# Re-planning the last blocks of an LSTM + state-space kernel, with a polynomial logarithm and one scan per piece

## The reference

```python
def layer0(x, h0, Wx, Wh, b):            # LSTM over 512 steps, hidden 512
    xW = x @ Wx + b
    for t in range(512):
        i, f, o, g = split(xW[:, t] + h @ Wh)        # sigmoid, sigmoid, sigmoid, tanh
        c = f * c + i * g
        h = o * tanh(c)
def layer1(x, conv_w, conv_b, Wp, bp, Ws, bs, A_log, dt_log, Wo, bo):   # conv_w = cond, 8 taps
    conv = conv_b + sum(x_pad[:, k:k + L] * conv_w[k] for k in range(8))
    proj = conv @ Wp + bp
    B, C = softplus(proj[..., :64]), tanh(proj[..., 64:])
    u = x @ Ws + bs
    decay = 1 - softplus(dt_log) * softplus(A_log)
    state[t] = decay * state[t-1] + softplus(dt_log) * B[t] * u[t]
    return (C * state) @ Wo + bo
x = x + layer0(x, cond, ...)
out = x + layer1(x, cond[:, None], ...)
```

## Time and profile before

| | |
|---|---|
| median of 3 runs | 1922.39 us (1920.68 to 1922.65) |
| profiled execution | 1919.75 us |
| its span, first to last instruction | 1917.8 us |
| granted TensorE clock, mean | 0.995 |
| busy: PE, PE weight load, DVE, ACT, POOL | 94%, 74%, 72%, 53%, 18% |

### The profile page before, as it was taken

One profiled execution on the slowest core, in us unless ns is written; L12 is line 12 of the kernel. 1 busy time (PEld: TensorE's weight loads), 2 busy tenths in 40 slices (PEclk: granted clock), 3 DMA queues, 4 the chain that ended last, 5 costly groups with the idle time before them and its releaser, 6 DMA issues.

```text
span 1917.8 us, 123272 instructions
## 1 busy us (share of the span) xinstructions
PE 1810.3 (94%) x52690; PEld 1419.5 (74%) x52690; DVE 1388.6 (72%) x6911; ACT 1015.9 (53%) x4057; POOL 337.5 (18%) x1544
## 2 busy tenths in 40 slices
PE   5888999999999999999999999999999999999976
PEld 3666777777777777777777777777777777777865
DVE  8677667777677776777777677777777777867675
ACT  5555455555555555555555545555555555545442
POOL 1111111111111111111111111111111111111110
PEclk9999999999999999999999999999999999999998
DMA  6111111111111211111111111111111121211100
GB/s 236 53 42 38 48 54 37 51 55 44 53 51 39 63 43 54 44 50 55 48 57 40 54 54 42 59 45 51 53 53 45 46 56 40 74 38 50 46 15 24
DMA packets 112668, 100.81 MB, mean 53 GB/s; under 512 B 20353, under 2 KB 86453, under 8 KB 111094
## 3 DMA queue, kind: packets, MB, share of 16 engines
q1 hardware_dynamic: 111704, 90.79, 15.6%
q10 hardware_dynamic: 416, 2.13, 0.3%
HBM read 50.90 MB, written 41.94 MB: 48 GB/s over the span
## 4 chain that ended last, share of the span: by engine, by line
PE 78%; DVE 10%; ACT 5%; issue 3%; POOL 2%; DMA 1%; SPq 0%; ACTq 0%; POOLq 0%; DVEq 0%
PE recA L540 28%; PE recB L534 24%; PE pw L501 12%; PE pbc L585 10%; DVE tr L900 4%; ACT act L783 3%; POOL h L468 2%; DVE hz L931 2%; DVE pre L906 2%; DVE prod L914 1%; ACT tc L793 1%; PE pw L485 1%; PE po L605 1%; PE pu L558 1%; DMA wpk<-in_L_cond_Wh_dram 1%
## 5 line engine op out<-in xcount | busy, mean ns | idle before, releaser
L783 ACT ACTIVATE act<-pre 128x64 f32<-128x64 f32 x1024 | 262.7, 257 | 854.3 <-DVE pre L909 838.1
L540 PE MATMUL recA<-whi,hz 128*16 128x256 f16 x8176 | 516.0, 275 | 75.6 <-DVE hz L931 62.3
L534 PE MATMUL recB<-whi,hz 128*32 128x128 f16 x16352 | 577.6, 219 | 0.4 <-issue 0.4
L534 PE MATMUL recB<-wlo,hz 128*32 128x128 f16 x16352 | 577.6, 219 | 0.1
L540 PE MATMUL recA<-wlo,hz 128*16 128x256 f16 x8176 | 512.6, 273 | 0.0
L534 PEld LDWEIGHTS recB<-whi,hz 128*32 128x32 f16 x16352 | 438.0, 97 | 10.2 <-issue 0.6
L534 PEld LDWEIGHTS recB<-wlo,hz 128*32 128x32 f16 x16352 | 437.9, 97 | 2.6 <-issue 0.2
L540 PEld LDWEIGHTS recA<-whi,hz 128*16 128x16 f16 x8176 | 199.9, 88 | 303.5 <-DVE hz L931 281.6
L900 DVE STREAM_TRANSPOSE tr<-recA 128x256 f32<-128x256 f32 x512 | 230.0, 449 | 203.5 <-PE recA L540 201.6
L585 PE MATMUL pbc<-yt,wpk 128*128 128x256 f32 (+5 forms) x1120 | 329.6, 400 | 0.0
L468 POOL TENSOR_TENSOR h<-osc,tc 128x16 f32<-128x16 f32 x1024 | 226.3, 221 | 465.4 <-ACT tc L793 465.4
(11 more groups left out here) (157 smaller groups left out, 1989.8 us busy)
## 6 DMA issues: line engine op xcount, KB each, us to landing
xw_rows<-xs SPq DMA_DIRECT2D x128, 256.0 KB, 2.5
seed<-xw_rows SPq DMA_DIRECT2D x1008, 32.0 KB, 2.0
xn<-in_x_dram SPq DMA_DIRECT2D x32, 256.0 KB
out_dram<-ot SPq DMA_DIRECT2D x32, 256.0 KB, 3.0
seed<-in_L_cond_Wh_dram ACTq DMA_DIRECT2D x2, 1024.0 KB, 6.6
wpk<-in_L_cond_Wh_dram SPq DMA_DIRECT2D x2, 1024.0 KB, 12.2
wlo<-in_L_cond_Wx_dram SPq DMA_DIRECT2D x2, 1024.0 KB, 13.7
xs<-in_L_cond_Wx_dram SPq DMA_DIRECT2D x1, 1024.0 KB, 10.0
```

Source lines behind the costliest of these rows:

```text
L534: ins = pe.matmul(rec[1][32 * j:32 * j + 32, 0:128], h[:, k, 2 * NB * (1 - c):2 * NB * (1 - c) + 32], w[:, k, 4 * (2 + c) + j, :], start=F ...
L540: ins = pe.matmul(rec[0][32 * j:32 * j + 2 * NB, 0:256].rearrange("p (c f) -> p c f", c=2), h[:, k, 2 * NB:4 * NB], w[:, k, :, :].rearrang ...
L783: act_eng.activation(act[q][:, 0:G, :].rearrange("p g n -> p (g n)"), pre[q][:, :, :, :].rearrange("p g c b -> p (g c b)"), ACT.Tanh, scal ...
```

## The change

1. **Planning.** Blocks 12 and 13, block 14 and piece 15 get plans of their own (`NEAR_END`: conv parts, first `y_u` step, first step of the ScalarE ops, `room`). `MANY` is gone: VectorE ops go by booked costs everywhere, with a table of costs for 128-column pieces.
2. **Conv in halves.** Blocks 13 and 14 convolve 16 steps (128 columns) at a time: 64 jobs in place of 32, the first half starting before the block's y is complete. Other jobs per piece stay 32.
3. **y of the last step alone.** `output` runs for steps 508 to 510 at step 510 and for 511 alone (32 columns), and the last conv is split in three: what needs y to 507 (32 jobs), to 510 (16 jobs, issued at step 511), and step 511 (4 jobs of 8 columns). `y_u` of a piece is issued behind conv in `beside`; for the last piece it comes after the 4 jobs, and `abs`, `sig` go ahead of `u` on ScalarE.
4. **Polynomial logarithm.** log(1+e^-|z|) = -log(1-s) is a polynomial of degree 10 in s: `den`, `rcp`, `w`, `w2` go, terms rise from seven to nine.
5. **One scan for all batches.** `drive` writes `acc` batch-major (a transposed view), `carry` adds decay times the state before to the first step of each batch, and `dec` holds 0 there, so that one scan runs through several batches: 128 columns each, so two scans for a block and one for a 16-step piece in place of eight. `ys` reads the state through a transposed view.
6. The outputs of blocks 0 to 11 come out at other steps, since `ys` does; the first half of block 15 is put out at 509, T and T+1 (residual, the two matmuls), the second half after it.

```diff
-        DVE_COST = {"den": 0.33, "rcp": 0.46, "w": 0.34, "w2": 0.34, "top": 0.34, "term": 0.44, "sum": 0.44,
-                    "drive": 0.44, "scan": 0.2, "ys": 0.35}
+        DVE_COST = {"top": 0.34, "term": 0.44, "sum": 0.44,
+                    "drive": 0.44, "carry": 0.1, "scan": 0.4, "ys": 0.35}
+        DVE_COST_HALF = {"top": 0.25, "term": 0.32, "sum": 0.32, "drive": 0.38, "carry": 0.2, "scan": 0.46, "ys": 0.3}
...
         def conv_order(i):
             n, a, e, cols = span(i)
+            taps = [(c, k) for k in range(TAPS) for c in range(KC)]
+            if i < LAST - 1:
+                return [(c, k, a, e) for c, k in taps]
             if i < NP - 1:
-                return [(c, k, a, e) for k in range(TAPS) for c in range(KC)]
-            reach = [min(e, e - HS + TAPS - 1 - k) for k in range(TAPS)]
-            return ([(c, k, a, reach[k]) for k in range(TAPS) for c in range(KC)] +
-                    [(c, k, reach[k], e) for k in range(TAPS) for c in range(KC) if reach[k] < e])
...
+                return [(c, k, lo, lo + TT) for lo in range(a, e, TT) for c, k in taps]
+            order, done = [], [a] * TAPS
+            for last in (e - HS, e - 1, e):
+                reach = [min(e, last + TAPS - 1 - k) for k in range(TAPS)]
+                order += [(c, k, done[k], reach[k]) for c, k in taps if done[k] < reach[k]]
+                done = reach
+            return order
...
+        NEAR_END = {LAST - 2: ([(0, 8, 3, 1), (8, 32, 11, 2)], 11, 23, 0.65),
+                    LAST - 1: ([(0, 64, -5, 3)], 10, 17, 0.65),
+                    LAST: ([(0, 32, -12, 3), (32, 64, 0, 3)], 4, 11, 0.9),
+                    LAST + 1: ([(0, 32, 0, 7)], 2, 5, 0.8)}
...
+            if i == NP - 1:
...
+                conv_when[i] = [(0, late[0], T - HS, (late[0] + HS - 1) // HS), (late[0], final[0], T - 1, jobs),
+                                (final[0], jobs, T, jobs)]
+                u_when[i] = [T] * KC
+                post_at[i] = [T + 1] * len(post_order(i))
...
-                    pe_load[first + (j - lo) // rate] += 0.46
+                    pe_load[first + (j - lo) // rate] += 0.46 if span(i)[3] == COLS and i < LAST - 1 else 0.23
...
                 if name == "drive":
                     dve.wait_ge(s_sp, i + 3)
                     dve.wait_ge(s_usb, i + 1)
-                    dve.scalar_tensor_tensor(sp[:, 0:cols], sp[:, 0:cols], dtv[:, 0:1], us[:, 0:cols],
-                                             ALU.mult, ALU.mult).then_inc(s_drive, 1)
+
+                    dve.scalar_tensor_tensor(by_batch(acc[:, 0:cols]), by_step(sp[:, 0:cols]), dtv[:, 0:1],
+                                             by_step(us[:, 0:cols]), ALU.mult, ALU.mult).then_inc(s_drive, 1)
+                elif name == "carry":
+
+                    if i:
+                        dve.wait_ge(s_drive, 2 * i)
+                        dve.wait_ge(s_scan, i)
+                        ahead = pieces[i - 1][2] - pieces[i - 1][1]
+                        first = acc[:, 0:cols:e - a]
+                        dve.scalar_tensor_tensor(first, st[:, (i - 1) % 2, ahead - 1:NB * ahead:ahead], decay[:, 0:1], first,
+                                                 ALU.mult, ALU.add).then_inc(s_drive, 1)
                 elif name == "scan":
...
+                    some = slice(128 * z, 128 * z + 128)
+                    ins = dve.tensor_tensor_scan(st[:, i % 2, some], dec[0 if e - a == TB else 1][:, :], acc[:, some], 0.0,
                                                  ALU.mult, ALU.add)
```

More of the change, by code:

```diff
@@ L190, in span, with y_steps, y_done @@
             return n, a, e, NB * (e - a)
+        def y_steps(t):
+            if t == T - 2:
+                return list(range(T - HS, T - 1))
+            if t == T - 1:
+                return [t]
+            return list(range(t - HS + 1, t + 1)) if (t + 1) % HS == 0 else []
+        def y_done(t):
+            return t // HS + 1 if t < T - 1 else T // HS + 1
         def conv_order(i):
             n, a, e, cols = span(i)
+            taps = [(c, k) for k in range(TAPS) for c in range(KC)]
+            if i < LAST - 1:
+                return [(c, k, a, e) for c, k in taps]
             if i < NP - 1:
[L197 to L205 removed]
+                return [(c, k, lo, lo + TT) for lo in range(a, e, TT) for c, k in taps]
[5 more added lines that the diff above has]
+            return order
         def soft_order(key):
[L208 removed]
+            return ["abs", "sig", "pos"], ["top"] + ["term"] * SERIES + ["sum"]
         def post_order(i):
             on_act, on_dve = soft_order(i + 2)
[L212 removed]
+            on_act = ["u"] + on_act + ["c"] if i < NP - 1 else ["abs", "sig", "u", "pos", "c"]
+            return on_act + on_dve + ["drive", "carry"] + ["scan"] * (span(i)[3] // 128) + ["ys"]
         par_order = sum(soft_order(0), []) + ["dtv"] + sum(soft_order(1), []) + ["dtv", "decay"]
@@ new lines, in lstm_ssm_kernel @@
+            base = TB * n + e
+            if i == NP - 1:
+                late = [j for j in range(jobs) if y_done(TB * n + min(e, conv_order(i)[j][3] + conv_order(i)[j][1] - TAPS + 1) - 1)
+                        > (T - HS) // HS]
+                final = [j for j in late if conv_order(i)[j][3] + conv_order(i)[j][1] - TAPS + 1 == e]
+                conv_when[i] = [(0, late[0], T - HS, (late[0] + HS - 1) // HS), (late[0], final[0], T - 1, jobs),
+                                (final[0], jobs, T, jobs)]
+                u_when[i] = [T] * KC
+                post_at[i] = [T + 1] * len(post_order(i))
+                slot = T + 2
+                continue
@@ new lines, in lstm_ssm_kernel @@
+            if i in NEAR_END:
+                conv_plan, u_first, slot, room = NEAR_END[i]
+                conv_when[i] = [(lo, hi, base + first, rate) for lo, hi, first, rate in conv_plan]
+                u_when[i] = [base + u_first + k for k in range(KC)]
+                slot += base
+            else:
+                conv_when[i] = [(0, 13, base + 3, 1), (13, 21, base + 16, 2), (21, jobs, base + 20, 1)]
+                u_when[i] = [base + 27 + k for k in range(KC)]
+                slot, room = base + 31, 0.65
@@ new lines, in lstm_ssm_kernel @@
+            act_at = ACT_AT if e - a == TB else {"u": 0, "abs": 0, "sig": 0, "pos": 1, "c": 1}
+            post_at[i] = [slot + act_at[name] for name in post_order(i)[:len(act_at)]]
+            slot += max(act_at.values())
+            for name in post_order(i)[len(act_at):]:
+                cost = (DVE_COST if e - a == TB else DVE_COST_HALF)[name]
+                while dve_load[slot] + cost > room:
+                    slot += 1
+                dve_load[slot] += cost
+                post_at[i].append(slot)
@@ L265, in lstm_ssm_kernel @@
+            slot += 3 if i not in NEAR_END else 0
+            for z in range(2):
+                if TT * z < e and a < TT * z + TT and (a <= TT * z):
+                    slot = min(slot + 3, T - 1)
                     while evacuates(slot):
                         slot += 1
[L267 to L287, removed]
+                    out_when[n, z] = (slot - 2, slot - 1, slot) if e - a == TB else (slot - 2, T, T + 1)
@@ L611, in beside @@
                 for i in range(NP):
+                    for lo, hi, first, rate in conv_when[i]:
+                        for j in due(t, first, rate, hi - lo):
+                            conv(i, lo + j)
                     for k in range(KC):
@@ L1058, in _ @@
             dve.memset(ys[N:N + 1, :, :], 1.0).then_inc(s_ones, 1)
-            dve.memset(dec[:, :], 1.0).then_inc(s_dec, 1)
+            for z in range(2):
+                dve.memset(dec[z][:, :], 1.0).then_inc(s_dec, 1)
+            dve.wait_ge(s_dec, 2)
+            for z in range(2):
+                dve.memset(dec[z][:, 0:128:TB >> z], 0.0).then_inc(s_dec, 1)
             for q in range(2):
```

107 lines of the change are left out of this document (35 added, 72 removed).

## The result

The changed kernel takes 1926.10 us (median of 22 runs, 1923.18 to 1928.76), the kernel before in the same sessions 1921.93 (22 runs, 1919.99 to 1927.47). The ratio is 1.0022, 95% interval [1.0016, 1.0027]: slower by 4.2 us, where I had forecast 1.3 us less, and above the high end of my range, 1925.0.

A forecast was written before the change was run, and what follows sets the result against it. A loop through VectorE, ScalarE and GpSimd sets the floor, TensorE the fuller steps; 10.5 + 1.5 - 10.8 - 2.5 = -1.3 us on the median 1922.39 gives 1921.1, range 1910.5 to 1925.

The forecast's parts named there:

- The threshold: Each step: side work is free down to a floor of 3.56 us, until TensorE's jobs overfill it; 0.03 us room.
- the lists: Jobs of each step worked out from the code, priced by trace durations to tell which steps exceed the floor.
- the middle costs nothing: Rival: fuller steps before the end cost no time, so its gain of 13.3 stays; 1910.6 us, chance 0.14.
- half of it: Rival: the additional job costs, but steps with output matmuls stay at the floor; 1915.8 us, chance 0.12.
- my likeliest case: Whole kernel: no change by the bound of 0.2%, 1921.1 us, own range 1918 to 1924, chance 0.67.
- The middle: Even groups 6 to 26: outputs moved earlier pack TensorE's steps fuller, 0.96 us per group, 11 groups: +10.5 us.
- Steps 416 to 479: Steps with half conv jobs or two conv jobs come to 5.5 us over the floor, in place of 4.0: +1.5.
- The end: Steps 480 to 510: gains of 2.6, 7.2 and 1.0 us in three stretches, together -10.8.
- the half clock stretch: Steps 493 to 507: TensorE's stretch at half its clock goes, since no step keeps it idle as long.
- The tail: From step 511's conv on: gains of 0.6 before `abs`, 1.24 in the series, 0.7 after `drive`; -2.5 us, give or take 1.
- My 0.115 a record: Last conv in the tail: price of each TensorE record in us, putting the end of 56 records at 1903.6.
- The transposed view: `drive`'s strided write on VectorE: bounds 0 and 1 ns a column; 0 taken, 0.5 us kept for the range.

The follow-up runs named there:

- the first kernel: The changed kernel with `y_u` issued ahead of the conv jobs again, except for the last piece; 1922.61 us, ratio 0.9999 to the kernel before.
- the third: The changed kernel with `y_u` ahead of conv and the outputs of blocks 0 to 10 at the steps of the kernel before; 1913.70 us, ratio 0.9949.
- fifth: The third with the last conv in two parts in place of three; 1911.11 us, ratio 0.9943 to the kernel before.
- the ninth: The fifth with 64 waits more on VectorE at its start; 1912.62 us, ratio 0.9941 to the kernel before.

## Why the prediction was wrong

**The threshold was right.** A step costs nothing until TensorE's jobs fill it, and the earlier trace rows showed 0.03 us of room. Five projections gave 3.67 (forecast 3.68), two conv jobs, or a conv and an output job, with three 3.63 to 3.65 (forecast 3.64), in the very steps that the lists named. Moving `ys`, and with it the outputs, cost 11.3 in the kernel with the polynomial alone and 9.9 in the first, against my 10.5. In the changed kernel it is 10.7: its 13.0 less the 2.3 of `y_u` below. The rivals "the middle costs nothing" and "half of it" are refuted by the same rows.

**The step that failed is the costing of one edit in the third part of the change, "`y_u` of a piece is issued behind conv".** It has no term in my sum. My lists counted each job of a step at its own duration, `y_u` at 0.37 wherever it stands, so that an exchange of two neighbours in one queue cost nothing. It costs 0.2 in every step where `y_u` and a later wide job are at the threshold: one of `y_u`'s four steps in each of the 11 blocks (219: 3.77, with `y_u` ahead 3.57), 428 to 430 and others. In steps 64 to 415 that is 11 x 0.21 = 2.3. The table's 13.0 - 9.9 = 3.1 has 0.8 more, since the first kernel's profile has a floor 0.007 higher, and the steps that TensorE fills are as long in both. In 416 to 479 it is 1.1 (428 to 430 and 458 to 460), in 480 to 492 0.6: 4.0 in all, of the 7.6 by which the two spans differ from the forecast. By the medians the first experiment gives back 3.5 of the missing 5.5, and without this one reordering the change measures 1922.6, inside the range of my likeliest case (1918 to 1924).

**The middle, +15.0 for 10.5.** 13.0 of it is in the table, 2.3 of that `y_u`'s; 2.0 is pauses, 0.5 of them VectorE's at 128n + 63 and 1.3 in steps 186 and 187, where the chain of the changed kernel shows issue, a wait for nothing that the profile shows, within recB:

```profile
721.41 0.33 PE recB L549 x21
721.74 0.55 issue
722.29 0.68 PE recB L549 x35
```

The first kernel loses 0.8 in the same two steps, the third and fifth 0.2 in 187, the others nothing; what such a stop is stays open.

**Steps 416 to 479, +3.1 for 1.5.** 1.1 of the 1.6 between them is `y_u` behind conv, and 0.36 more is step 461 with 3.93, a pause of VectorE at a record 128n + 63: the first kernel has it too, and in the ninth, whose records are shifted, the step lasts 3.57. The prices held: three half jobs and four projections have the 3.68 of the forecast, and steps 431 to 437, with two conv jobs of a whole block and four projections, or a transpose or residual and two or three, last 3.75 to 3.87, the 0.2 to 0.3 over the floor that I had given them.

**The end, -9.3 for -10.8.** 493 to 507 came to 54.54 for "near 54.0"; the half clock stretch of the earlier trace rows is gone, as forecast (granted 1.00 from 1870 to 1880). The 0.8 missing in 480 to 492 is mostly `y_u` behind conv again, 0.6.

**The tail, -1.7 for -2.5.** From `abs` to `drive` 5.40 became 1916.44 - 1912.27 = 4.17, a gain of 1.23 for the 1.24 forecast. From `drive` to the matmuls 1.59 for 1.38: `carry` has 0.23 and the scan 0.43, within my bounds, and `drive` 0.43 for 0.38. The gain of 0.6 ahead of `abs` is zero: 7.22 us pass from the first conv record to `abs`, and 7.23 did before. My 0.115 a record held for the full clock (48 records in 5.49, 56 in the third kernel's 6.36, which would be a gain of 0.7); that the clock falls within the small jobs was in my text as a risk of 1 us and should have been in the sum, since I had read the 2.08 of the last output matmuls as half clock already, without asking where ahead of them it begins.

**The transposed view** costs 0.7 ns a column, inside the bounds of 0 and 1, and nearer to the end that I didn't take. From the groups after:

```profile
L1007 DVE SCALAR_TENSOR_TENSOR acc<-sp,dtv,us 64x256 f32<-64x256 f32 x15 | 9.9, 659 | 0.0
L1032 DVE TENSOR_TENSOR ys<-ct,st 64x256 f32<-64x256 f32 x15 | 8.9, 596 | 0.0
```

659 - 477 = 182 ns for 256 columns of `drive`, and 596 in place of 417 for `ys`. The Trainium skill (SBUF — State Buffer, section Door 1: The DMA port swizzle) says that fp32 accesses which leave a 16-byte line each time pay a penalty. These two rows agree, in write and in read.

**The range.** Its high end took 0.5 for the view and 2 for the middle above the forecast. An edit that I listed and didn't price had no share in it.

## What to carry to other kernels

When an engine's queue is full to within 0.03 us of a threshold, an edit that only reorders it, or that makes hidden work finish earlier and so moves what waits for it, has to be priced like added work: print the steps that each job lands in before and after. Price a job by its neighbours, not by itself: on TensorE count the changes from narrow weights to wide ones in a step, and put the narrow jobs next to each other (here `y_u` first or last, not in between). Of two such losses in the same steps, undo both before judging either: alone they gave back 3.5 and 4.3 us, together 12.4, and with them and the shorter tail the change is 0.57% faster than the kernel before, not 0.22% slower.

## What the runs showed of the hardware that I had not expected

- A TensorE job with weights of 128 columns costs 0.2 us more behind one with 32 or 64 columns than behind another of 128: conv 0.63 against 0.43, two projections 0.67 against 0.47. Weight loads in the groups after:

```profile
L600 PEld LDWEIGHTS pbc<-yt,wpk 128*128 128x128 f32 x1256 | 180.7, 190 | 45.9
...
L494 PEld LDWEIGHTS px<-ident,xn 128*128 128x128 f32 x128 | 18.2, 145 | 7.8 <-DMA xn<-in_x_dram 2.0
...
L573 PEld LDWEIGHTS pu<-yt,ws 128*64 128x64 f32 x272 | 13.6, 140 | 18.9 <-issue 17.5
```

  The Trainium skill (TensorE: Matmul & The Clock Gate, section LDWEIGHTS (loading the stationary operand)) has the time of a load go by its columns. The rows agree in part: 190 ns for conv's 128 columns against 140 for `y_u`'s 64, but the transposes of x load 128 columns in 145. Nor are 50 ns the 0.2 us. What the first wide job waits for wasn't measured.
- VectorE is late by up to 0.37 us at records 128n + 63 of its stream. In 352 steps it passes 47 or 48 of them, and 15 to 22 show in a step's length. Whether it pauses so in an execution that isn't profiled, no run here shows. One of the kernel before, on its timeline, is the second `hz` (L925):

```profile
440.20 0.22 ACT L793 ACTIVATE tc<-act 128x16 f32<-128x16 f32 x1
...
440.44 0.17 DVE L925 TENSOR_TENSOR hz<-osc,tc 128x16 f16<-128x16 f32 x1
...
443.81 0.21 ACT L793 ACTIVATE tc<-act 128x16 f32<-128x16 f32 x1
...
444.21 0.17 DVE L925 TENSOR_TENSOR hz<-osc,tc 128x16 f16<-128x16 f32 x1 [0.25 <-ACT tc L793]
```

  It starts 0.24 after `tc` does in the one step, and 0.40 after it in the next, which lasts 3.75. Other instructions ahead on VectorE move these pauses, so single steps of two kernels don't compare.
- The floor isn't the same in each execution: it is 3.563 in the profiles of before and after, 3.570 in the first kernel's, 3.571 in the ninth's. 0.007 in 512 steps is 3.6 us. So the profile of the first kernel has a span only 1.2 below the changed one's, while the medians differ by 3.5; time over an execution's own floor is what two profiles can be compared by.
